# 128-wide linear attention: the eight PSUM banks shared out as 2, 5 and 1, and the output projection issued in two halves

## What is computed

```python
q = _rope(split(x @ wq.T, 16 heads)); k = _rope(split(x @ wk.T, 4 heads)); v = split(x @ wv.T, 4 heads)
k, v = repeat(k, 4), repeat(v, 4)
def step(kv, inp):                       # one chunk of the sequence
    qi, ki, vi = inp
    scores  = (qi @ ki.T) * diag         # decay inside the chunk
    o_intra = scores @ vi
    o_inter = (qi * q_dec) @ kv
    kv      = blk * kv + (ki * k_dec).T @ vi
    return kv, o_intra + o_inter
x = x + (concat heads of o) @ wo.T       # the output projection, 2048 -> 256
```

## Time and profile before

| | us |
|---|---|
| median of three runs | 3156.69 |
| the profiled execution, its own time | 3153.1 |
| its span, first to last instruction | 3150.4 |
| this layer in it, from its first product to the next layer's first | 540.2 (750.30 to 1290.53) |
| one turn of it, the second | 133.88 (885.57 to 1019.45) |
| mean granted TensorE clock of the span | 0.926 of full speed |

### The profile page before, as it was taken

The page is one execution under the profiler, slowest core; times in us unless marked ns, Lnnn a source line. Parts: engine busy times, 40 slices in busy tenths (PEclk is TensorE's granted clock), DMA queues, the critical chain, the costliest instruction groups (busy, mean ns, idle before and its releaser), DMA issues. The chain is left out here.

```text
span 3150.4 us, 45793 instructions
## 1 busy us (share of the span) xinstructions
PE 2854.7 (91%) x15592; PEld 1944.5 (62%) x15592; DVE 1659.8 (53%) x4517; ACT 842.7 (27%) x1368; POOL 992.2 (31%) x1105
## 2 busy tenths in 40 slices
PE   7999999998999999999979999999999758888876
PEld 3444458886656555788867777777777634443444
DVE  5566646666555646466644333333333565555555
ACT  2343344442101101344422222222222002222310
POOL 0000036765444445567631122222221011121211
PEclk8999999999999999999989999999999657888975
DMA  3000020000000000100000000000000000000000
GB/s 138 1 0 0 0 100 1 0 0 0 1 0 0 0 0 0 81 0 0 0 14 14 1 14 15 14 1 14 15 1 1 24 0 1 1 0 1 1 0 27
DMA packets 6288, 37.96 MB, mean 12 GB/s; under 512 B 272, under 2 KB 4368, under 8 KB 4496
## 3 DMA queue, kind: packets, MB, share of 16 engines
q1 hardware_dynamic: 6160, 36.34, 3.0%
HBM read 34.24 MB, written 2.10 MB: 12 GB/s over the span
## 5 line engine op out<-in xcount | busy, mean ns | idle before, releaser
L590 PE MATMUL banks<-back 32*128 32x512 f32 (+3 forms) x1088 | 364.6, 598 | 31.4 <-DVE back L600 22.1
L365 PE MATMUL banks<-moe_parts 128*128 128x512 f32 x1536 | 368.4, 396 | 15.3 <-POOL moe_parts L445 8.5
L817 ACT ACTIVATE back<-banks 128x1024 f32<-128x1024 f32 (+3 forms) x256 | 217.0, 863 | 459.7 <-PE banks L711 459.5
L365 PEld LDWEIGHTS banks<-moe_parts 128*128 128x128 f32 x1536 | 287.7, 191 | 78.5 <-issue 20.8
L1433 PE MATMUL banks<-lin_parts 128*128 128x512 f32 x1152 | 307.5, 413 | 18.9 <-DVE lin_parts L1684 15.5
L1619 DVE TENSOR_TENSOR ffn_pack<-banks,back 128x512 f32<-128x512 f32 x128 | 88.5, 691 | 351.5 <-PE banks L1446 351.4
L711 PE MATMUL banks<-back 32*128 32x512 f32 (+3 forms) x1024 | 242.3, 586 | 19.8 <-DVE back L833 12.5
L1433 PEld LDWEIGHTS banks<-lin_parts 128*128 128x128 f32 x1152 | 213.6, 194 | 67.4 <-issue 21.0
L590 PEld LDWEIGHTS banks<-back 32*128 32x128 f32 x1088 | 135.2, 199 | 187.9 <-DVE back L604 77.8
L1749 POOL TENSOR_TENSOR ffn_pack<-ffn_pack 128x256 f32<-128x256 f32 x112 | 82.9, 740 | 498.9 <-ACT ffn_pack L1582 498.9
L604 DVE TENSOR_REDUCE back<-banks 128x1 f32<-128x512 f32 x272 | 176.5, 687 | 79.9 <-PE banks L590 75.4
(11 more groups left out here) (235 smaller groups left out, 5307.0 us busy)
## 6 DMA issues: line engine op xcount, KB each, us to landing
back<-p_raw SPq DMA_DIRECT2D x8, 1024.0 KB, 4.8
back<-p SPq DMA_DIRECT2D x1, 7696.0 KB, 21.5
ffn_pack<-ffn SPq DMA_DIRECT2D x1, 6144.0 KB, 26.8
back<-p SPq DMA_DIRECT2D x1, 5152.0 KB, 15.2
back<-p SPq DMA_DIRECT2D x2, 1792.0 KB, 8.2
out<-x SPq DMA_DIRECT2D x1, 2048.0 KB, 7.5
x<-x_in SPq DMA_DIRECT2D x1, 1536.0 KB, 12.7
small_pack<-small SPq DMA_DIRECT2D x1, 619.0 KB, 4.9
```

The costliest lines, as they stand in the source:

```text
L365: mm = nc.tensor.matmul(bank[:], up[:, n % 2, a, which, kd, :], xp[:, b, kd, :], start=((a, b, kd) == (0, 0, 0)), stop=((a, b, kd) == (1, ...
L590: nc.tensor.matmul(bank[:, 0:n], qs[head_rows[j], hg, qi * P:(qi + 1) * P], ks[head_rows[j], hg, 0:n], start=True, stop=True).then_inc(D.f ...
L817: nc.scalar.activation(pt[:, (kt % 2) * 2 + pair, :, q0:T], two[:, :, q0:T], ACT.Exp, scale=0.25).then_inc(A.free.s, 2)
```

## The change

Ring A gets banks 0 and 1, ring D banks 2 to 6, ring O bank 7; after the layer ring A gets its four banks back. `project` and `add_output` now do one half of a projection for each call, and are called in the steps n = 0 (half 0) and n = 1 (half 1) of the next group; after the last step both halves of group 3 follow each other as before. No operation of any engine is added, removed or resized.

```diff
-    D.take(c.banks[4:6])
-    O.take(c.banks[6:8])
+    A.take(c.banks[0:2])
+    D.take(c.banks[2:7])
+    O.take(c.banks[7:8])
...
-                def project(g):
-                    pe.wait_ge(A.free.s, A.released(it, "out", g, NT - 1))
-                    for half in range(2):
-                        pe.wait_ge(O.free.s, O.may_fill(it))
-                        bank = O.fill("y", g, half)
+                def project(g, half):
+                    if half == 0:
+                        pe.wait_ge(A.free.s, A.released(it, "out", g, NT - 1))
+                    pe.wait_ge(O.free.s, O.may_fill(it))
+                    bank = O.fill("y", g, half)
...
-                    if n == 0 and g:
-                        project(g - 1)
+                    if n < 2 and g:
+                        project(g - 1, n)
...
                 turn_xn(nc, c, pe, it)
-                project(G3 - 1)
+                for half in range(2):
+                    project(G3 - 1, half)
...
-                def add_output(g):
-                    for half in range(2):
-                        dve.wait_ge(O.full.s, O.may_read(it))
+                def add_output(g, half):
+                    dve.wait_ge(O.full.s, O.may_read(it))
...
-                    if n == 0 and g:
-                        add_output(g - 1)
+                    if n < 2 and g:
+                        add_output(g - 1, n)
                 keep_xt(nc, c, dve, it)
-                add_output(G3 - 1)
+                for half in range(2):
+                    add_output(G3 - 1, half)
...
     now.close()
+    A.take(c.banks[0:4])
```

More of the change, by code:

```diff
@@ L1107, in output @@
                     mm.then_inc(A.full.s, 1)
-                def project(g):
-                    pe.wait_ge(A.free.s, A.released(it, "out", g, NT - 1))
-                    for half in range(2):
-                        pe.wait_ge(O.free.s, O.may_fill(it))
-                        bank = O.fill("y", g, half)
[L1114 to L1119, removed]
+                def project(g, half):
[3 more added lines that the diff above has]
+                    bank = O.fill("y", g, half)
+                    for i in range(2 * half, 2 * half + 2):
+                        for h in range(HQ):
+                            mm = nc.tensor.matmul(bank[:, (i % 2) * DM:(i % 2 + 1) * DM],
+                                                  ot[:, h, i * P:(i + 1) * P], wo[:, g * HQ + h, :],
+                                                  start=(h == 0), stop=(h == HQ - 1))
+                    mm.then_inc(O.full.s, 1)
                 for what in first_products:
@@ L1196, in keep_state @@
                             .then_inc(D.free.s, 1)
-                def add_output(g):
-                    for half in range(2):
-                        dve.wait_ge(O.full.s, O.may_read(it))
[L1201 to L1206, removed]
+                def add_output(g, half):
+                    dve.wait_ge(O.full.s, O.may_read(it))
+                    bank = O.read("y", g, half)
+                    if g:
+                        dve.wait_ge(O.free.s, O.released(it, "y", g - 1, half))
+                    xs = c.x[:, it, 2 * half:2 * half + 2, :]
+                    nc.vector.tensor_tensor(xs, xs, bank[:].rearrange("p (a d) -> p a d", a=2), ALU.add)\
+                        .then_inc(O.free.s, 1)
                 for what in first_products:
```

## The result

The changed kernel took 3114.83 us (median of four runs, 3109.91 to 3117.34) where the kernel before took 3156.43 (3152.51 to 3158.48): a ratio of 0.9868, 95% interval 0.9851 to 0.9885. The forecast was 3129.1 with a range of 3121 to 3142. The direction was right, the time lies outside the range: 41.6 us were gained, not 27.6. The profiled execution of the changed kernel took 3116.7 us with a span of 3114.9, against 3153.1 and 3150.4.

What follows compares the result with a forecast made beforehand. TensorE's own work was taken as the bound, only its gaps winnable. 9.19 - 1.86 = 7.33 us a turn, 29.3 in four, plus 1.7, minus 3.4, gives 27.6: 3156.7 to 3129.1 us, range 3121 to 3142.

Steps and rivals of the forecast that it cites:

- The bound and the gaps: Two-product steps: TensorE's work bounds the layer; more ring D banks and the halved projection win 9.19 us a turn.
- The thin margins: Replayed steps: qd, ACT's copy and DVE's addition are ready 0.4 to 1.4 us before TensorE wants them.
- The single bank of ring O: Group 3 and turn's end: half 1 waits for DVE's addition of half 0, 0.75 and 1.11, costing 1.86 us a turn.
- The scores of the turn's start: Turn's start: first scores start as late as before, 14.02 us in; TensorE's idle time becomes one 3.06 us pause.
- The clock in the layer: Third turn's half clock goes, winning 1.7 us; the new turn-start pause brings it in two of four turns, costing 3.4 us.
- Later layers are unchanged in work, 3 us either way: Layers behind this one: same work, slow clock stretches may shift, 3 us allowed either way.
- The measure: Whole kernel: the median of the runs stays 3.6 us above the profiled execution, as before.
- DVE or POOL as the bound: Rival in the steps: late data halves the 9.19 us win, 11 us gained in all, 3146 us; chance 0.12.
- no effect: Rival in the gaps: they are data waits in disguise, so the time stays at 3157 us; chance 0.03.
- slower by ring O: Rival in steps (1,1) and (2,1): the single bank blocks TensorE behind DVE's queue, 11 us slower, 3168 us; chance 0.04.
- The rival of the clock: Rival at the turn's start: the long pause costs the clock every turn, for longer, 17.5 us gained, 3139 us; chance 0.10.

Runs made afterwards that it cites:

- E4: Changed kernel with rings A, D, O at 2, 4 and 2 banks and the turn-end transposed tiles through ring O, halves kept: 3123.02 us, ratio 0.9901.
- E9: Changed kernel plus a pure delay behind this layer, a block of four DVE reductions with results unused: 3134.83 us, ratio 0.9932.
- E3: Kernel before with rings A, D, O at 2, 4 and 2 banks, projection whole, turn-end transposed tiles through ring O: 3121.38 us, ratio 0.9892.
- E10: Changed kernel plus a delay block ahead of this layer, one DVE reduction over 1024 columns: 3130.75 us in one execution.
- E11: Changed kernel plus a delay block ahead of this layer, one DVE reduction over 2048 columns: 3123.82 us in one execution.
- E12: E3 with rings A, D, O at 3, 3 and 2 banks, projection whole: 3121.63 us in one profiled execution.
- E1: The changed kernel again, no edit, with more executions: 3122.25 us, ratio 0.9898 to the kernel before.

## Why the prediction missed, step by step

- **The bound and the gaps, right.** 9.19 us of pauses a turn in four steps: steps (0,0), (0,1) and (1,1) came out at 6.01, 6.90 and 10.36 us, forecast 6.0, 6.9 and 10.4. The thin margins held; no matmul's wait for qd, state or ACT's copy came up beside the 0.76 us ahead of `project` in group 3, which was there before.
- **The single bank of ring O, right.** 1.86 us a turn were forecast; 0.52 and 0.78 us of named idle time came, with release and slow start 0.78 and 1.04 us where 0.75 and 1.11 were forecast; 7.38 us net a turn (133.88 - 126.50) where 7.33 was worked out. E4 shows that the bank is the cause.
- **The scores of the turn's start, right.** 13.98 us where 14.02 was kept, and a pause of 3.01 us where 3.06 was forecast.
- **The clock in the layer, mechanism right, size off.** Two falls were taken for 3.4 us, one came: the first turn's step (0,0) lost 1.7 us. Over the eight profiles of kernels that have this pause, 15 of 32 turns fell, so two in four was a fair mean, but the falls are not drawn one by one: in these eight profiles either all four turns fell, or the first alone, or none. Also, in the kernel before the slow stretch around 750 us lay on this layer's first products, 15.4 us to the scores, and in the changed kernel it fell ahead of them, 14.1 us. In the working's terms, two falls at 1.7 us were taken off and one came (1.7 us to the good), and the first products and the turns gave 1.3 and 0.2 us that it did not have: 3.2 us together. The layer's 30.8 us are 4 x 7.37, plus 1.7 for the third turn, minus 1.7 for the first, plus 1.3 for its products; the 1.5 us by which the layer began later take back this last.
- **"Later layers are unchanged in work, 3 us either way": the step that failed.** Their work is unchanged, but their clock isn't. In the pair of profiles they gave 6.3 us. The next two layers' part, 1.4 and 2.0 us, came in both profiles of the changed kernel, and was gone in E9. That it belongs to where these layers begin is likely but not shown, by the two weak points named there. The rest, 2.9 us, is the last stage, which runs at a mean clock of about 0.75 (0.59 to 0.89 over stretches of 100 us in the profile after). Up to its last TensorE instruction it took between 637.9 and 648.9 us over all fourteen profiles, the same kernel 637.9 and 644.9. I had seen 6 us between three runs of before and allowed only half of it.
- **The measure: a second term that failed.** The working kept the 3.6 us by which the median of before stood above its profiled execution. For the changed kernel the median stands 1.9 us below it, and with the 3.3 us of the four runs of before that makes the 5.2 us. The changed kernel's first four executions (3110 to 3117) lie in the faster part of its nine (3109 to 3126). The second set has it at 3122.25, inside the forecast range; but the median of all nine is 3116.7, still below it, and 39 us under the median of the 13 executions of before in the two sets. So luck of the first four is only a part of the miss. The range should have been the working's 27.6 us plus what the executions of either kernel spread, some 8 us on each side.
- **Rivals.** DVE or POOL as the bound, no effect and slower by ring O did not come. The rival of the clock came in E3, E4 and E10, with 1.4 to 3.1 us a turn, not in the changed kernel. The Trainium skill ("TensorE: Matmul & The Clock Gate", "HAM oscillation — how this bites in real kernels") tells of waits of about 3 to 5 us for a DMA, behind each of which the next burst begins cold. I took that over to a pause of 3.0 us, at the lower end of it; so taken, all turns would pay. Three kernels here agree (E3, E4, E10), E11 and E12 do not, and the changed kernel only in its first turn.

**What stays open.** I have shown that a delay can bring these falls in this layer, not which start gives which outcome: E11 began its layer 3 us later than E1 and had the same turns two to four. How much of the last stage's spread follows its start, and how much differs by execution for one and the same kernel, no run here tells apart; at least 7 us do the latter. So of the 41.6 us, 31 lie in this layer (29.5 in its turns' pauses, most of the rest in a slow stretch that moved out of its first products), about 3 in the two layers behind it, probably by its shift, and the rest can't be told from the spread of executions.

## What to carry to other kernels

Replay a ring fill by fill with the trace's own prices, and ask of each pause whether the bank or the data behind it would have come first; here that gave the turn to 0.05 us (126.55 worked out, 126.50 measured). Look for independent work to put between before asking for banks: half a projection in the right step won two thirds of a turn's gain, and two products put into the longest pause won a further 10 us in the layer. Where one kernel's executions spread by 0.5%, as here, a change of 1% cannot be forecast closer than that, and a comparison of two variants needs the time of the changed stretch from the profile beside the total.

## What was not expected of the hardware

The same pause of 3.02 us in the same instructions brought the half clock (1.2 GHz) in every turn of one kernel, at 1.4 to 3.1 us a time, and never in another that begins 0.4 us later (E10, E11). Many falls repeat from execution to execution: the third turn of the kernel before took 135.56 us in three profiles of three, the 64-wide layer of the changed kernel 870.8 and 870.9 us in two of two. Not all do: the first turn of before fell in one profile of three, and its 64-wide layer took 872.8, 875.0 and 873.1 us. So a fall at a given place is often, not always, the same in every execution of a program, and in the last stage executions of one kernel part by 7 us.
